# Attention and FP4 feed-forward on one core: output tiles in three PSUM banks, six residual buffers, and other places and lengths for the last two pairs' key sums

## The chip, the cores and the metric

The kernel runs on one core of a Trainium2 chip. The metric is device time in microseconds (us). The kernel before has a median of 3647.8 us over three runs (3647.26 to 3649.82).

## The reference

x is (8, 1024, 512), eight batches. Everything is float32.

```python
xn = _layernorm(x, axis=-1)
x = x + _L0_attn_ref(xn, W_attn, b_attn, W_proj, b_proj) + _L0_ffn_ref(xn, w_gate, w_up, w_down)

# attention: 16 heads of 32, causal
qkv = x @ W_attn + b_attn
att = jnp.einsum('bhqd,bhkd->bhqk', q, k) * HD ** (-0.5)
att = jax.nn.softmax(jnp.where(causal, att, -jnp.inf), axis=-1)
y = jnp.einsum('bhqk,bhkd->bhqd', att, v)
return y @ W_proj + b_proj

# feed forward: every operand rounded to blocks of 16 FP4 values with a common scale
h = jax.nn.silu(fp4_linear(x, w_gate)) * fp4_linear(x, w_up)
return fp4_linear(h, w_down)
```

## The kernel before, in words

The attention of all eight batches comes first (to about 2077 us of the span), then the feed-forward over 64 tiles of 128 rows. The change is in the attention, and its effects reach the first steps of the feed-forward.

A batch has three stages. In the first TensorE makes Q, K and V (line 1056, three products of rounded halves each). In the second it goes through eight pairs of heads, numbered 0 to 7 in the code. In the third, the output projection, it makes eight output tiles of 128 rows, "P0" to "P7" (line 1227). Each output tile is the sum over four groups of heads; a group is one matmul of the program and two instructions in the trace. Groups 0 to 2 need pairs 0 to 5, group 3 needs pairs 6 and 7.

**A pair.** TensorE computes the transposed scores of one key tile after the other (kt = 0 to 7, L1113). ScalarE writes their exponentials (L967 and L970). TensorE multiplies them with V (`times_v`, L1139). GpSimd adds the exponentials of the key tiles up: L613 adds tiles 0 and 1, and L615 adds tiles 2, 3, ... one by one. ScalarE copies the first 128 columns (L962). `denominators(p)` then multiplies these sums with ones on TensorE (L1151), and where GpSimd added only `summed(p)` tiles, it adds the remaining tiles' exponentials with further matmuls (L1158). For pairs 0 to 5 GpSimd adds all eight tiles. For pair 6 it adds five (kt = 0 to 4), for pair 7 three. The sums of pairs 1 and 3 lie in `xs`, those of all others in `stage`. So pair 7's first sum waits until the denominators of pair 6 have read `stage`.

For pairs 0 to 6 the denominators are issued in the middle of the next pair's steps, and their inverse goes through DMAs. For pair 7 they come last: VectorE takes the reciprocal from PSUM directly (L709) and divides (L720).

**The order around the projection.** All engines but SP issue in an order written out in the code. On TensorE, after the denominators of pair 7: the transposes of three tiles of the next batch's x (L1014), groups 0 to 2 of P0 and P1, the transpose of the fourth x tile, group 3 of P0 and P1, then P2 and P3 whole, the transposes of a quantised weight unit (L1098, `transpose_unit`), P4 and P5, those of a second unit, P6 and P7, and then the next batch's Q and K. P_k lies in bank k mod 2 of `ps_dense`, so P2 waits until VectorE has added P0 (`o_sum`).

On VectorE: four normalisations of the next batch's x (L645) in the middle of pair 7, the divisions of pair 6, the reciprocal and divisions of pair 7, `low_of_x` of the four x tiles (L651), and then `add(k)` for k = 0 to 7 (L731), with the quantisation of two weight units in between: after `add(0)` the scales of the first unit (L760 to L764), after `add(1)` its rounding (L770 to L774), after `add(2)` and `add(3)` the same for the second, after `add(4)` and `add(6)` their low halves (L780). The fourth `low_of_x` needs the fourth transpose. `transpose_unit` needs the end of the rounding (L774) of its unit, and for the second also the low half of the first.

`add(k)` also needs x plus the bias: ScalarE's queue loads a tile of x into one of two buffers (L935), and GpSimd adds the bias (L603). The first two loads are issued once the denominators of pair 7 are done, each later one after `add(k)` has freed its buffer.

In the last batch there is no next x to normalise and transpose; a tile of the feed-forward's x is quantised instead (L1360, L1553), and SP loads 18 weight blocks after `add(1)`.

Of the kernel before, what the change touches and what calls it, by code (L numbers as in the profile page):

```python
# [44 lines left out]
def attention(nc, ctx, banks, memory, shared, x, w_attn, b_attn, w_proj, b_proj, w_gate, w_up, w_down, qk_scratch, ones_scratch,  # L45
# [27 lines left out]
    ST_RING, SLOTS, XR = 3, 4, 4  # L73
# [10 lines left out]
    def summed(p):  # L84

        return ST if p < PAIRS - 2 else RINGED if p < PAIRS - 1 else 3
# [5 lines left out]
    SUMS0 = [sum(summed(k) - 1 for k in range(p)) for p in range(PAIRS)]  # L92
    SUMS = SUMS0[-1] + summed(PAIRS - 1) - 1
# [72 lines left out]
    stack01 = sb("stack01", [P, 2, 4, S], F32R)  # L166
    arena = sb("arena", [P, 2, KC, S], F32R)
# [73 lines left out]
    res_in = [sem(f"a_res_in{i}") for i in range(2)]  # L241
# [11 lines left out]
    ONE = 1  # L253
    LOOPED = [*x_in, bn_part, bn_tile, var_eps, rstd, normed, kept, d_full, t_full, t_hi, t_lo, qk_hi, qk_lo, *qk_out,
# [4 lines left out]
    LOADS = 7  # L259

# [9 lines left out]

    def bank(kind, i):
        return ps_dense[:, DN[kind, i] % 2]
# [9 lines left out]

    X_SUMS = (1, 3)
    SUMMED_IN = {p: max((k for k in range(p) if (k in X_SUMS) == (p in X_SUMS)), default=None) for p in range(PAIRS)}

    def sums(p, h):
        return both_sums(p)[:, h]

    def both_sums(p):
        if p in X_SUMS:  # L290
            return xs[:, :, :].rearrange("p (h a) n -> p h (a n)", h=2)
        return stage[:, :, :, :].rearrange("p h a n -> p h (a n)")
# [95 lines left out]

    def batches(eng, body):

        with eng.Fori(0, B - 1) as b:
            body(b, False)
        body(B - 1, True)
# [177 lines left out]
    def gpsimd(pool):  # L571
# [25 lines left out]
        def body(b, final):  # L597
            for t in range(XR, ST):
                inv_std(b, t)

            def x_and_bias(t):
                pool.wait_ge(res_in[t % 2], ONE + b * (ST // 2) * DMA + (t // 2 + 1) * DMA)
                nc.gpsimd.tensor_tensor(res[:, t % 2], res[:, t % 2], bp[:, :], ALU.add).then_inc(o_res, 1)  # L603

            def sum_up(p, kt):

                pool.wait_ge(st_exp, ONE + b * PAIRS * NPARTS + p * NPARTS + PART0[kt + 1])
                if kt > 1:
                    pool.wait_ge(summed_up, ONE + b * SUMS + SUMS0[p] + kt - 1)
                both = both_sums(p)  # L610
# [19 lines left out]
        batches(pool, body)  # L630

    def vector(dve):
# [45 lines left out]
        def body(b, final):  # L678
# [44 lines left out]
            def add(k):  # L723
# [7 lines left out]
                nc.vector.tensor_tensor(ob[:, k % 2], bank("P", k), res[:, k % 2], ALU.add).then_inc(o_sum, 1)  # L731
# [146 lines left out]
    def scalar(act):  # L878
# [14 lines left out]
        def body(b, final, rest):  # L893
# [37 lines left out]
            def load(k):  # L931

                t = OUT[k]
                act.wait_ge(o_sum, ONE + b * ST + max(k - 1, 0))
                act.dma_start(res[:, k % 2], x[b, t * P:(t + 1) * P, :]).then_inc(res_in[k % 2], DMA)  # L935
# [8 lines left out]
            for p in range(PAIRS):  # L944
                for kt in range(ST):
# [7 lines left out]
                    if kt == RINGED:  # L953
# [8 lines left out]
                        nc.scalar.activation(both_sums(p)[:, :, 0:P], exps(0)[:, :, 0:P], ACT.Copy).then_inc(first_sums, 1)  # L962
# [16 lines left out]
            for k in range(2):  # L979
                load(k)  # L980
# [6 lines left out]
            for k, t in enumerate(OUT):  # L987
                act.wait_ge(o_sum, ONE + b * ST + k + 1)
                act.dma_start(acc[b, t * P:(t + 1) * P, :], ob[:, k % 2]).then_inc(o_out[k % 2], DMA)
                if k + 2 < ST:  # L990
                    load(k + 2)
# [14 lines left out]
    def tensor(pe):  # L1006
# [20 lines left out]
        def body(b, final):  # L1027
            def emptied(kind, i):

                n = DN[kind, i] - 2  # L1030
# [6 lines left out]
                s, per = {"QK": (qk_lo, NQK), "V": (v_done, ST), "P": (o_sum, ST)}[k]  # L1037
# [105 lines left out]
            def denominators(p):  # L1143
                pe.wait_ge(summed_up, ONE + b * SUMS + SUMS0[p] + summed(p) - 1)
# [4 lines left out]
                for s in range(2):  # L1149
                    for h in range(2):  # L1150
                        last = nc.tensor.matmul(by_tile(den_bank(p)[y_rows(h, s)]), ones[:, :], by_tile(sums(p, h))[:, s::2],  # L1151
                                                start=True, stop=summed(p) == ST)
                for kt in range(summed(p), ST):
# [80 lines left out]
            for k in range(2):  # L1234
                pe.wait_ge(y_div, ONE + b * PAIRS * 2 + (PAIRS - 2 + k) * 2)
# [6 lines left out]
            for k in range(ST):  # L1242
                if k < 2:
# [23 lines left out]

    def x_read(eng):
# [3 lines left out]
    shared.wgu_in, shared.wd_in = wgu_in, wd_in  # L1272
    shared.all_quantised, shared.all_added, shared.projected, shared.x_read = all_quantised, all_added, projected, x_read
# [3 lines left out]
def feed_forward(nc, ctx, memory, shared, x, F, acc, wq, out):  # L1277
# [280 lines left out]
    def tensor(pe):  # L1558
# [26 lines left out]
        def step(t, first=False, second=False, last=False):  # L1585
            pe.wait_ge(xt_lo, t + 1)
            if first:
                pe.wait_ge(shared.wgu_in, len(PIECES) * DMA)
            else:
# [103 lines left out]
```

## Time and profile before

| | us |
|---|---|
| median of the runs | 3647.8 |
| the profiled execution, its own time | 3647.5 |
| its span, from the first to the last instruction | 3645.7 |
| mean granted TensorE clock | 0.997 of full speed |
| TensorE busy | 3597.6 (99%) |
| VectorE busy | 2610.7 (72%) |
| GpSimd busy | 1078.4 (30%) |

A busy share says little here, since matmuls overlap in the records. What counts is the stretch between the last pair of one batch and the first Q of the next, which comes once in each of the eight batches. The rows below show it in the second batch, where it runs from about 488 to 536 us. The same steps in the first batch stand between 234 and 282 us, in the eighth between 2024 and 2077 us.

### The profile page before, as it was taken

The page shows a single profiled execution, that of the slowest core. Times are in us where ns is not written, and L with a number is a line of the kernel's source. Part 1 is how long each engine was busy: PE and PEld are TensorE (multiplying, and loading weights), DVE is VectorE, ACT ScalarE, POOL GpSimd, SP SyncE. Part 2 cuts the span into 40 slices and gives each one's busy share as a digit, 9 for nine tenths or more (in the row PEclk, how much of TensorE's full clock was granted, in tenths as well). Part 3 has the DMA queues.
Part 4 walks back from the last instruction along what each step waited for, and adds up shares of the span by engine and source line. Part 5 has one row for each costly group of instructions (what it writes and reads, how often), then busy time and mean ns, then how long its engine had stood idle before and what let it go on. Part 6 is the DMA issues. An engine that isn't in the chain of part 4 may idle for free.

```text
span 3645.7 us, 55788 instructions
## 1 busy us (share of the span) xinstructions
PE 3597.6 (99%) x20748; PEld 2604.6 (71%) x20748; DVE 2610.7 (72%) x3834; ACT 1193.0 (33%) x2249; POOL 1078.4 (30%) x542
## 2 busy tenths in 40 slices
PE   8999999999999999999999999999999999999999
PEld 6557557566566575575565588888888888888887
DVE  6776766766767767767667577777777777777776
ACT  2542533533524515425325322222222222222222
POOL 0760952833825717608518300000000000000000
PEclk9999999999999999999999999999999999999999
DMA  6525436336255255254355500111011101110110
GB/s 195 133 77 183 110 115 177 83 119 181 64 168 150 66 186 129 80 183 101 120 167 156 202 26 29 35 35 32 29 35 35 32 29 35 35 32 29 35 35 29
DMA packets 180445, 336.13 MB, mean 92 GB/s; under 512 B 42688, under 2 KB 50368, under 8 KB 179392
## 3 DMA queue, kind: packets, MB, share of 16 engines
q1 hardware_dynamic: 156096, 280.47, 27.1%
q10 hardware_dynamic: 24192, 53.49, 4.3%
q8 instruction: 108, 1.77, 0.2%
q14 instruction: 49, 0.40, 0.0%
HBM read 213.92 MB, written 118.43 MB: 91 GB/s over the span
## 4 chain that ended last, share of the span: by engine, by line
PE 90%; issue 3%; POOL 2%; DVE 2%; DMA 1%; ACT 1%; SPq 0%; POOLq 0%; ACTq 0%; DVEq 0%
PE f_ps L1570 26%; PE ps_dense L1056 13%; PE f_ps_o L1582 13%; PE ps_st L1113 8%; PE ps_s L1081 5%; PE ps_dense L1227 5%; PE ps_y L1139 4%; PE ps_dense L1139 3%; PE ps_dense L1081 2%; PE ps_dense L1151 2%; PE f_ps L1562 1%; POOL stage L615 1%; PE ps_st L1122 1%; PE ps_s L1086 1%; POOL stage L613 1%
## 5 line engine op out<-in xcount | busy, mean ns | idle before, releaser
L1570 PE MATMUL f_ps<-wgu,xqt 128*128 128x512 f32 (+1 forms) x4608 | 992.7, 373 | 1.4 <-DVE xqt L1430 1.4
L1570 PEld LDWEIGHTS f_ps<-wgu,xqt 128*128 128x128 f32 x4608 | 842.5, 188 | 122.7 <-DVE xqt L1430 1.7
L967 ACT ACTIVATE pt<-ps_st 128x512 f32<-128x512 f32 (+3 forms) x1152 | 540.8, 525 | 489.9 <-PE ps_st L1113 335.3
L683 DVE TENSOR_REDUCE mx<-ps_s 128x1 f32<-128x640 f32 (+3 forms) x512 | 524.1, 1024 | 164.2 <-PE ps_s L1086 163.6
L1582 PE MATMUL f_ps_o<-wd,hqt 128*128 128x512 f32 x2112 | 513.4, 396 | 0.2 <-DVE hqt L1456 0.2
L1582 PEld LDWEIGHTS f_ps_o<-wd,hqt 128*128 128x128 f32 x2112 | 392.6, 189 | 79.5 <-DVE hqt L1456 0.6
L1056 PE MATMUL ps_dense<-arena,wa 128*128 128x512 f32 x1536 | 384.3, 400 | 0.0
L615 POOL TENSOR_TENSOR stage<-stage,pt 128x1536 f32<-128x1536 f32 (+2 forms) x128 | 378.9, 2960 | 16.6 <-ACT pt L967 6.3
L613 POOL TENSOR_TENSOR stage<-pt 128x1792 f32<-128x1792 f32 x48 | 192.7, 4014 | 615.9 <-ACT pt L967 563.9
L1056 PEld LDWEIGHTS ps_dense<-arena,wa 128*128 128x128 f32 x1536 | 281.9, 189 | 58.0 <-issue 3.8
L683 DVE TENSOR_REDUCE mx<-ps_dense 128x1 f32<-128x128 f32 (+3 forms) x424 | 204.4, 482 | 90.5 <-PE ps_dense L1086 90.5
L1113 PE MATMUL ps_st<-arena 98*128 98x512 f32 (+3 forms) x768 | 254.8, 401 | 4.0 <-DMA arena<-mr 2.1
L1113 PE MATMUL ps_st<-stack 98*128 98x512 f32 (+3 forms) x768 | 254.6, 397 | 0.4 <-ACT pt L967 0.2
L1227 PE MATMUL ps_dense<-wp,yt 128*128 128x512 f32 x512 | 227.5, 594 | 2.7 <-DVE rob L731 2.3
L1517 ACT ACTIVATE silu<-f_ps 128x512 f32<-128x512 f32 (+1 forms) x192 | 106.9, 557 | 369.1 <-PE f_ps L1570 369.1
L929 ACT ACTIVATE stage<-ps_dense,bqk 128x512 fp32r<-128x512 f32 x128 | 87.9, 687 | 351.6 <-PE ps_dense L1056 343.0
L1512 ACT ACTIVATE ha<-ht 128x1408 f32<-128x1408 f32 x63 | 87.1, 1383 | 325.3 <-DVE ht L1353 325.3
L1449 DVE TENSOR_TENSOR h<-silu,f_ps 128x512 f32<-128x512 f32 (+1 forms) x192 | 122.7, 639 | 95.6 <-ACT silu L1517 91.8
L1056 PE MATMUL ps_dense<-wa,arena 128*128 128x512 f32 x768 | 188.2, 395 | 0.0
L1113 PEld LDWEIGHTS ps_st<-arena 98*128 98x128 f32 x768 | 130.9, 193 | 77.3 <-ACT pt L967 41.3
L1227 PEld LDWEIGHTS ps_dense<-wp,yt 128*128 128x128 f32 x512 | 94.0, 190 | 113.8 <-issue 102.8
L736 DVE SCALAR_TENSOR_TENSOR stage<-ps_dense,bqk,stage 128x512 fp32r<-128x512 f32 x128 | 95.9, 749 | 105.7 <-ACT stage L929 105.7
(145 smaller groups left out, 5295.1 us busy)
## 6 DMA issues: line engine op xcount, KB each, us to landing
qk_scratch<-stage SPq DMA_DIRECT2D x128, 512.0 KB, 2.8
stack<-qk_scratch SPq DMA_DIRECT2D x192, 256.0 KB
arena<-qk_scratch SPq DMA_DIRECT2D x192, 256.0 KB
xs<-in_L_attn_x SPq DMA_DIRECT2D x64, 256.0 KB, 3.9
rob<-in_L_attn_x ACTq DMA_DIRECT2D x64, 256.0 KB, 2.9
acc_scratch<-rob ACTq DMA_DIRECT2D x64, 256.0 KB, 2.1
xt<-in_L_attn_x SPq DMA_DIRECT2D x64, 256.0 KB, 2.6
at<-acc_scratch SPq DMA_DIRECT2D x64, 256.0 KB, 2.7
```

Of the source, the lines that this page charges most:

```text
L613: nc.gpsimd.tensor_tensor(both[:, :, cols], exps(0)[:, :, cols], exps(1), ALU.add).then_inc(summed_up, 1)
L615: nc.gpsimd.tensor_tensor(both[:, :, cols], both[:, :, cols], exps(kt), ALU.add).then_inc(summed_up, 1)
L683: nc.vector.tensor_reduce(mx[:, h * ST + q:h * ST + q + 1], scores_bank(p, n)[:, 0:(q + 1) * P], axis=AX.X, op=ALU.max, negate=True).then_ ...
L967: nc.scalar.activation(exps(kt)[:, heads[0], q - kt * P:q - kt * P + n], ps_st[:, w % ST_RING, 0:n], ACT.Exp, scale=SCALE).then_inc(st_exp, 1)
L1056: last = nc.tensor.matmul(bank(*use), left(lh, k), right(rh, k), start=n == 0, stop=n == len(terms) - 1)
L1081: nc.tensor.matmul(out[:, k0:k1], qs, stack(p)[0:KS, 2 + h, k0:k1], start=True, stop=k1 < keys)
L1113: last = nc.tensor.matmul(ps_st[:, w % ST_RING, j * n:(j + 1) * n], stack(p)[0:KM, 2 + h, kt * P:(kt + 1) * P], stack(p)[0:KM, h, q:q + n] ...
L1139: last = nc.tensor.matmul(by_tile(y_bank(p)[y_rows(h, s), y_cols(kt, s)]), v_head(kt, p, h), exps_of_parity(kt, h, s), start=kt == 0, stop ...
L1227: last = nc.tensor.matmul(bank("P", k), yt[:, g, t * P:(t + 1) * P], wp[:, g, :], start=g == 0, stop=g == G - 1)
L1449: nc.vector.tensor_tensor(h[:, f:f + n], silu[:, c, 0:n], ps[:, SLOT[c], 1, 0:n], ALU.mult).then_inc(h_mul, 1)
L1570: last = nc.tensor.matmul(ps[:, SLOT[c], gu, 0:n].rearrange("p (j n) -> p j n", n=P), xqt[:, a, k], wgu[:, b, gu * FC + f // P:gu * FC + ( ...
L1582: last = nc.tensor.matmul(ps_o[:, :], hqt[:, a, k], wd[:, b, k], start=i == 0, stop=i == len(terms) - 1)
```

## The change

Four things change.

- **Three banks.** P_k goes to bank k mod 3 of `ps_dense[0]`, `ps_dense[1]` and the second half of `ps_s`. TensorE issues groups 0 to 2 of P0, P1 and P2 ahead of the fourth x transpose. P3 is the first that waits for `add(0)`. This holds in all eight batches.
- **Six residual buffers.** In all but the last batch, x tiles are loaded into six buffers, the two of `rob` and four in `stage`. Six loads are issued at once after the denominators of pair 7, and the last two after `add(0)` and `add(1)`.
- **Sums.** In all but the last batch, pair 6's sums lie in `left01`, which is what pairs 4 and 5 have left in `stack01`. So pair 7's first sum no longer waits for the denominators of pair 6. Pair 7 has five tiles summed in place of three.
- GpSimd's batches are written out in line and no longer in a loop, and the feed-forward's first matmuls wait also for `add(5)` of the last batch, since they use the third bank.

```diff
+    ST_RING, SLOTS, XR, RES = 3, 4, 4, 6
-    def summed(p):
-        return ST if p < PAIRS - 2 else RINGED if p < PAIRS - 1 else 3
+    def summed(p, final):
+        return ST if p < PAIRS - 2 else 3 if p == PAIRS - 1 and final else RINGED
...
+    left01 = memory.over("left01", [P, 2, 4, S], F32, "stack01")
...
+    def res_tile(k, final):
+        i = res_place(k, final)
+        return res[:, i] if i < 2 else stage[:, :, :, :].rearrange("p a c n -> p (a c) n")[:, i - 2]
+    def res_place(k, final):
+        return k % 2 if final else k % RES
...
+    OUT_BANKS = 3
     def bank(kind, i):
+        if kind == "P":
+            return [ps_dense[:, 0], ps_dense[:, 1], ps_s[:, QC:S]][i % OUT_BANKS]
...
+    def sums_place(p, final):
+        return 1 if p in X_SUMS else 2 if p == PAIRS - 2 and not final else 0
+    def summed_in(p, final):
+        return max((k for k in range(p) if sums_place(k, final) == sums_place(p, final)), default=None)
...
-                if SUMMED_IN[p] is not None:
-                    pool.wait_ge(den_full, ONE + b * PAIRS + SUMMED_IN[p] + 1)
-                for kt in SUM_ORDER[:summed(p) - 1]:
+                if summed_in(p, final) is not None:
+                    pool.wait_ge(den_full, ONE + b * PAIRS + summed_in(p, final) + 1)
+                for kt in SUM_ORDER[:summed(p, final) - 1]:
                     sum_up(p, kt)
...
-            for k in range(2):
+            for k in range(2 if final else RES):
                 load(k)
...
+                if kind == "P" and i >= OUT_BANKS:
+                    pe.wait_ge(o_sum, ONE + b * ST + i - OUT_BANKS + 1)
+                    return
...
-            for k in range(2):
-                pe.wait_ge(y_div, ONE + b * PAIRS * 2 + (PAIRS - 2 + k) * 2)
+            for k in range(OUT_BANKS):
+                pe.wait_ge(y_div, ONE + b * PAIRS * 2 + (PAIRS - 2 + min(k, 1)) * 2)
                 emptied("P", k)
                 output(k, range(G - 1))
             if not final:
                 transpose_x(b + 1, XR - 1)
...
-                if k < 2:
+                if k < OUT_BANKS:
                     output(k, [G - 1])
```

TensorE's queue in the first batch, from the denominators of pair 7 to the first `transpose_unit`. Before (`ps_st<-ident,xs` are the x transposes, `ps_dense<-wp,yt` the output tiles, `ps_y<-ident,pt` the weight unit; a matmul here is two instructions of the trace):

```order
L1151 MATMUL ps_s<-stage,ones 32x512 [waits a_first_sums,a_summed_up]
L1151 MATMUL ps_s<-stage,ones 32x512 x3
L1158 MATMUL ps_s<-pt,ones 32x256 x2
L1158 MATMUL ps_s<-pt,ones 32x384 x2
L1158 MATMUL ps_s<-pt,ones 32x256 x4
L1158 MATMUL ps_s<-rob,ones 32x128 x2
L1158 MATMUL ps_s<-rob,ones 32x256 x2
L1158 MATMUL ps_s<-rob,ones 32x128 x6
```

After, the same place:

```order
L1180 MATMUL ps_s<-stage,ones 32x512 [waits a_first_sums,a_summed_up]
L1180 MATMUL ps_s<-stage,ones 32x512 x3
L1187 MATMUL ps_s<-rob,ones 32x128 x2
L1187 MATMUL ps_s<-rob,ones 32x256 x2
L1187 MATMUL ps_s<-rob,ones 32x128 x6
```

The eight matmuls on the exponentials of tiles 3 and 4 are gone, and the wait on `a_summed_up` is now for four sums and not for two. Further down on TensorE, before:

```order
L1227 MATMUL ps_dense<-wp,yt 128x512 [waits a_v_done,a_y_div,a_den_copy]
L1227 MATMUL ps_dense<-wp,yt 128x512 x2
L1227 MATMUL ps_dense<-wp,yt 128x512 [waits a_v_done,a_y_div]
L1227 MATMUL ps_dense<-wp,yt 128x512 x2
L1014 MATMUL ps_st<-ident,xs 128x128 [waits a_normed,a_t_lo]
L1014 MATMUL ps_st<-ident,xs 128x128 x3
L1227 MATMUL ps_dense<-wp,yt 128x512 [waits a_y_div]
L1227 MATMUL ps_dense<-wp,yt 128x512
L1227 MATMUL ps_dense<-wp,yt 128x512 [waits a_o_sum]
L1227 MATMUL ps_dense<-wp,yt 128x512 x3
L1227 MATMUL ps_dense<-wp,yt 128x512 [waits a_o_sum]
L1227 MATMUL ps_dense<-wp,yt 128x512 x3
L1098 MATMUL ps_y<-ident,pt 128x128 [waits a_q_q,a_q_lo]
```

After:

```order
L1256 MATMUL ps_dense<-wp,yt 128x512 [waits a_v_done,a_y_div]
L1256 MATMUL ps_dense<-wp,yt 128x512 x2
L1256 MATMUL ps_s<-wp,yt 128x512 [waits a_s_max,a_y_div]
L1256 MATMUL ps_s<-wp,yt 128x512 x2
L1036 MATMUL ps_st<-ident,xs 128x128 [waits a_normed,a_t_lo]
L1036 MATMUL ps_st<-ident,xs 128x128 x3
L1256 MATMUL ps_dense<-wp,yt 128x512 [waits a_y_div]
L1256 MATMUL ps_dense<-wp,yt 128x512
L1256 MATMUL ps_s<-wp,yt 128x512
L1256 MATMUL ps_dense<-wp,yt 128x512 [waits a_o_sum]
L1256 MATMUL ps_dense<-wp,yt 128x512 x3
L1127 MATMUL ps_y<-ident,pt 128x128 [waits a_q_q,a_q_lo]
```

Three matmuls of P2 now stand ahead of the fourth x transpose, where before there were none of them; `transpose_unit` still comes after P3. VectorE's queue has the same instructions in the same order in both.

## Rows read from the trace of the kernel before

**Rows 1.** The page: the chain of work that ended last, by engine.

```profile
PE 90%; issue 3%; POOL 2%; DVE 2%; DMA 1%; ACT 1%; SPq 0%; POOLq 0%; ACTq 0%; DVEq 0%
```

**Rows 2.** Who TensorE waited for, whole span (total us, times, longest us).

```profile
PE ps_dense L1227 <- DVE rob L731: 2.3, 8, 0.3
```

**Rows 3.** Timeline of TensorE, pair 7 (start us, duration us, what).

```profile
501.69 0.62 PE L1151 MATMUL ps_s<-stage,ones 128*32 128x512 f32 x2
505.02 1.53 PE L1014 MATMUL ps_st<-ident,xs 128*128 128x128 f32 x12
506.38 5.32 PE L1227 MATMUL ps_dense<-wp,yt 128*128 128x512 f32 x12
511.54 0.60 PE L1014 MATMUL ps_st<-ident,xs 128*128 128x128 f32 x4
511.97 1.88 PE L1227 MATMUL ps_dense<-wp,yt 128*128 128x512 f32 x4
514.15 7.13 PE L1227 MATMUL ps_dense<-wp,yt 128*128 128x512 f32 x16 [0.29 <-DVE rob L731]
521.12 0.60 PE L1098 MATMUL ps_y<-ident,pt 128*128 128x128 f32 x4
```

**Rows 4.** Timeline of GpSimd: sums of pair 7, a bias addition.

```profile
488.90 1.02 POOL L593 TENSOR_TENSOR mv<-mv,small 128x4 f32<-128x4 f32 x1
492.56 4.02 POOL L613 TENSOR_TENSOR stage<-pt 128x1792 f32<-128x1792 f32 x1 [2.63 <-PE ps_dense L1158]
496.65 3.46 POOL L615 TENSOR_TENSOR stage<-stage,pt 128x1536 f32<-128x1536 f32 x1
...
523.94 1.42 POOL L603 TENSOR_TENSOR rob<-rob,bp 128x512 f32<-128x512 f32 x1 [2.46 <-DMA rob<-in_L_attn_x]
```

**Rows 5.** Groups of GpSimd's instructions by shape (total us, mean ns | idle before).

```profile
L615 POOL TENSOR_TENSOR stage<-stage,pt 128x1280 f32<-128x1280 f32 x40 | 117.0, 2925 | 4.1
L615 POOL TENSOR_TENSOR stage<-stage,pt 128x1024 f32<-128x1024 f32 x40 | 95.3, 2382 | 3.5
```

**Rows 6.** Timeline of ScalarE: last exponentials of tile 1, and of tile 2, pair 7.

```profile
490.46 0.49 ACT L967 ACTIVATE pt<-ps_st 128x384 f32<-128x384 f32 x1
...
494.14 1.15 ACT L967 ACTIVATE pt<-ps_st 128x512 f32<-128x512 f32 x3 [2.70 <-PE ps_st L1113]
```

**Rows 7.** Timeline of TensorE and VectorE: denominators of pair 6, begin and end.

```profile
490.45 1.06 PE L1151 MATMUL ps_dense<-stage,ones 128*32 128x512 f32 x8
...
492.50 0.69 DVE L700 COPY rob<-ps_dense 128x512 f32<-128x512 f32 x1 [3.14 <-PE ps_dense L1158]
```

**Rows 8.** Timeline of VectorE, from the end of pair 7.

```profile
498.64 1.76 DVE L645 TENSOR_SCALAR xs<-xs,mv 128x512 f32<-128x512 f32 x1
505.20 3.36 DVE L709 RECIPROCAL rob<-ps_s 128x512 f32<-128x512 f32 x1 [0.21 <-PE ps_s L1158]
510.11 1.89 DVE L651 TENSOR_TENSOR arena<-ps_st,arena 128x512 fp32r<-128x512 f32 x3
513.41 0.68 DVE L731 TENSOR_TENSOR rob<-ps_dense,rob 128x512 f32<-128x512 f32 x1
519.32 0.69 DVE L774 TENSOR_TENSOR pt<-pt 128x512 f32<-128x512 f32 x1
524.27 1.65 DVE L771 SCALAR_TENSOR_TENSOR pt<-pt 128x512 f32<-128x512 f32 x1
527.16 0.68 DVE L780 TENSOR_TENSOR pt<-ps_y,pt 128x512 fp32r<-128x512 f32 x1
```

**Rows 9.** All normalisations (duration ns min/median/max, first and last start).

```profile
L645 DVE TENSOR_SCALAR xs<-xs,mv x64: 533/538/3444, 14.2 to 1824.4; 128x512 f32<-128x512 f32 x64
```

**Rows 10.** Timeline of TensorE, the last batch's projection.

```profile
2042.64 5.32 PE L1227 MATMUL ps_dense<-wp,yt 128*128 128x512 f32 x12
2048.37 9.14 PE L1227 MATMUL ps_dense<-wp,yt 128*128 128x512 f32 x20 [0.41 <-DVE yt L720]
...
2068.07 0.66 PE L1098 MATMUL ps_y<-ident,pt 128*128 128x128 f32 x4 [2.73 <-DVE pt L780]
```

More of the change, by code:

```diff
@@ L82, in attention @@
     TAIL = 2 * P * sum(ST - k for k in range(RINGED, ST))
-    def summed(p):
-        return ST if p < PAIRS - 2 else RINGED if p < PAIRS - 1 else 3
+    def summed(p, final):
+        return ST if p < PAIRS - 2 else 3 if p == PAIRS - 1 and final else RINGED
     SUM_ORDER = [*range(1, ST)]
     FREED = {0: 1, 1: 1, 2: 2, 3: 3, 4: 4}
-    SUMS0 = [sum(summed(k) - 1 for k in range(p)) for p in range(PAIRS)]
-    SUMS = SUMS0[-1] + summed(PAIRS - 1) - 1
+    SUMS0 = [sum(summed(k, False) - 1 for k in range(p)) for p in range(PAIRS)]
+    SUMS = SUMS0[-1] + summed(PAIRS - 1, False) - 1
     TILES = 2 * ST
@@ L240, in attention @@
     y_div = sem("a_y_div")
-    res_in = [sem(f"a_res_in{i}") for i in range(2)]
+    res_in = [sem(f"a_res_in{i}") for i in range(RES)]
     o_res = sem("a_o_res")
@@ L259, in attention, with res_turn @@
     LOADS = 7
+    def res_tile(k, final):
[3 more added lines that the diff above has]
+        return k % 2 if final else k % RES
+    def res_turn(b, k, final):
+        if final:
+            return b * 2 + k // 2 + 1
+        return b * 2 + k // RES + 1 if k % RES < 2 else b + 1
     LOADS_AFTER = {GROUP0 - 1: LOADS, 6: 1, 7: 1, 8: 1, 9: 1, 10: 2, 11: 1}
@@ L283, in attention, with sums, both_sums @@
     X_SUMS = (1, 3)
[L284 to L292, printed above, removed]
+    def sums_place(p, final):
+        return 1 if p in X_SUMS else 2 if p == PAIRS - 2 and not final else 0
+    def summed_in(p, final):
+        return max((k for k in range(p) if sums_place(k, final) == sums_place(p, final)), default=None)
+    def sums(p, h, final):
+        return both_sums(p, final)[:, h]
+    def both_sums(p, final):
+        return [stage[:, :, :, :].rearrange("p h a n -> p h (a n)"),
+                xs[:, :, :].rearrange("p (h a) n -> p h (a n)", h=2),
+                left01[:, :, 3]][sums_place(p, final)]
     def by_tile(a):
@@ L387, in attention @@
     NEEDS.update({("V", t): t + 1 for t in range(ST)})
[L389 to L393, printed above, removed]
     def batches_in_line(body):
@@ L609, in sum_up @@
                     pool.wait_ge(summed_up, ONE + b * SUMS + SUMS0[p] + kt - 1)
-                both = both_sums(p)
+                both = both_sums(p, final)
                 cols = slice(kt * P, S)
@@ L628, in body @@
                 x_and_bias(t)
-        batches(pool, body)
+        batches_in_line(body)
     def vector(dve):
@@ L730, in add @@
                 filled(dve, b, "P", k)
-                nc.vector.tensor_tensor(ob[:, k % 2], bank("P", k), res[:, k % 2], ALU.add).then_inc(o_sum, 1)
+                nc.vector.tensor_tensor(ob[:, k % 2], bank("P", k), res_tile(k, final), ALU.add).then_inc(o_sum, 1)
             def low_of_qk(i):
@@ L933, in load @@
                 t = OUT[k]
-                act.wait_ge(o_sum, ONE + b * ST + max(k - 1, 0))
-                act.dma_start(res[:, k % 2], x[b, t * P:(t + 1) * P, :]).then_inc(res_in[k % 2], DMA)
+                act.wait_ge(o_sum, ONE + b * ST + max(k + 1 - (2 if final else RES), 0))
+                act.dma_start(res_tile(k, final), x[b, t * P:(t + 1) * P, :]).then_inc(res_in[res_place(k, final)], DMA)
             for i in range(2):
@@ L989, in body @@
                 act.dma_start(acc[b, t * P:(t + 1) * P, :], ob[:, k % 2]).then_inc(o_out[k % 2], DMA)
-                if k + 2 < ST:
-                    load(k + 2)
+                if k + (2 if final else RES) < ST:
+                    load(k + (2 if final else RES))
                 if k == 0:
@@ L1150, in denominators @@
                     for h in range(2):
-                        last = nc.tensor.matmul(by_tile(den_bank(p)[y_rows(h, s)]), ones[:, :], by_tile(sums(p, h))[:, s::2],
-                                                start=True, stop=summed(p) == ST)
-                for kt in range(summed(p), ST):
+                        last = nc.tensor.matmul(by_tile(den_bank(p)[y_rows(h, s)]), ones[:, :], by_tile(sums(p, h, final))[:, s::2],
+                                                start=True, stop=summed(p, final) == ST)
+                for kt in range(summed(p, final), ST):
                     for s in range(2):
```

19 lines of the change are left out of this document (13 added, 6 removed).

## The prediction, made before the changed kernel ran

> **What bounds the kernel now.** I read the chain of work that ended last, then TensorE's waits, then the engines' timelines around the end of a batch. The chain is 90% TensorE [rows 1], so an edit pays only if it shortens what TensorE does or waits for. The only wait that the third bank can remove is TensorE's on `add(0)`, and it is booked with 2.3 us over eight batches [rows 2]. In the timeline it is a little more: the four instructions from 511.97 at 0.43 us each would end at 513.69, and the next start at 514.15 [rows 3]. That is 0.46 us a batch. The reader is to see how tight the neighbours are. The denominators of pair 7 start at 501.69, and GpSimd's last sum had ended at 496.65 + 3.46 = 500.11 [rows 3, 4]: 1.6 us of slack. The first `transpose_unit` starts at 521.12, and the rounding that it needs ended at 519.32 + 0.69 = 520.01 [rows 3, 8]: 1.1 us of slack. The change uses up both.
>
> **Step A, the denominators of pair 7 (seven batches).** Gain: eight matmuls less. Pair 6's denominators have exactly the list that pair 7's will have. They ran from 490.45 to VectorE's start at 492.50, 2.05 us [rows 7]; pair 7's ran from 501.69 to 505.20, 3.51 us [rows 3, 8]. So 1.46 us is saved.
>
> Cost: two more sums stand ahead. The exponentials of tile 1 are ready at 490.46 + 0.49 = 490.95, and GpSimd is free at 488.90 + 1.02 = 489.92 [rows 4, 6], so the first sum can start at 491.0 instead of 492.56, the part that waited for pair 6's denominators. It ends at 495.0. Tile 2's exponentials come at 494.14 + 1.15 = 495.29 [rows 6]; its sum runs from 495.35 to 498.82. The sums of tiles 3 and 4 take 2.92 and 2.38 us [rows 5] with 0.08 us between, so the last ends at about 504.3. TensorE had nothing else left at 501.69 and issues in order: it waits 2.65 us. Behind it stand the transposes of x and the whole projection. Net A = 2.65 - 1.46 = +1.2 us.
>
> **Step B, the first weight unit (seven batches).** The third bank puts six instructions (2.6 us) ahead of the fourth x transpose. VectorE's `low_of_x` of that tile comes ahead of `add(0)`, and everything of VectorE behind `add(0)` moves with it. From the first x transpose at 505.02, TensorE before: first `transpose_unit` at 521.12, 16.1 us later [rows 3]. After: 1.36 us of transposes (506.38 - 505.02), 18 instructions at 5.16/12 = 0.43 us, 7.74 us, to the fourth transpose; 1.87 us from there to `add(0)` (513.41 - 511.54); 6.60 us from `add(0)` to the end of the rounding (520.01 - 513.41) [rows 3, 8]. Together 17.57. Is VectorE itself free by then? It starts the reciprocal when the denominators end (505.20) and had done three `low_of_x` at 512.00, 6.8 us later [rows 8]; the fourth transpose comes after 9 us. So `transpose_unit`, which stays behind P3, has to wait for the rounding, and B = +1.5 us; the 0.46 us gap is already inside these figures. P3 itself doesn't wait: `add(0)` ends at 11.65, and P3 starts at 12.1.
>
> The second `transpose_unit` follows 17 instructions of 0.43 us (four transposes count as one) after the first, 7.3 us, at 24.9 on this scale. It needs the first unit's low half, which ended 14.43 us after `add(0)` (527.84 - 513.41), at 25.4. But in this stretch an L771 took 1.65 us beside a bias addition of GpSimd at 523.94 [rows 4, 8]. That addition followed a load that `add(2)` freed, and with six buffers it is gone by then. So 0 to 0.5 us, and I take 0. After it TensorE runs P6 and P7 as before, and the delay reaches Q and K of the next batch in full.
>
> **Step C, VectorE and GpSimd beside each other.** A normalisation takes 0.54 us alone, and up to 3.44 [rows 9]. In the second batch the first one is issued at 498.64, under the sum that ends at 500.11, and ends at 500.40 [rows 4, 8]: it waits for the end of GpSimd's instruction. Before, nothing of GpSimd stood behind this sum. Now two sums do. If a normalisation gets in between two sums, it delays the second by 0.54 us. Bounds from these rows: nothing (GpSimd is never held up) to 1.9 us (all four go ahead, the later ones 0.45 us apart). I take one in each of the two gaps, +1.1 us. The Trainium skill, SBUF — State Buffer, in the section on the two separate sides, says that the two engines share one pair of ports as an exclusive lock which is held for a whole instruction, by whichever starts first. By that rule, the row on the normalisation agrees, and the delay goes in both directions, so C would not be zero; it doesn't say who is next in a queue.
>
> **Other edits, at nothing.** Six loads in ScalarE's queue take some 2.6 us ahead of its x copies; those are wanted only by `low_of_x` after the reciprocal and the divisions, 5 us later. They also don't shorten a wait of TensorE, since only 2.3 us in all hung on `add` [rows 2]. Pair 6's sums start up to 1 us earlier, and its denominators did not wait for them. GpSimd's batches in line: it sits idle at each batch's start. The feed-forward's wait for `add(5)`: that is two tiles before TensorE gets there.
>
> **The last batch.** Its sums and buffers are as before; only the bank changes. P2's first groups run from about 2047.8 to 2050.4 instead of the wait until 2048.37, so group 3 of P0 starts 2.0 us later than at 2048.37 [rows 10]. `add(0)`, its loads and the roundings all move by 2.0. TensorE reaches the first `transpose_unit` at 2056.4 and waits for its rounding. The second was bound by VectorE already, 2.73 us of waiting for the low half at 2068.07 [rows 10], and that chain, from `add(2)` over a load, starts 2.0 later. So +2.0 us; bounds 1 (loads slow for reasons of their own) to 3.
>
> **Sum.** 7 x (1.2 + 1.5 + 1.1) + 2.0 = 28.6 us. The span of the profiled execution is 3645.7, and its own time 3647.5, 0.3 under the median. 3647.5 + 28.6 = 3676.1; by the median 3676.4. I forecast 3676 us, slower by 0.8%.
>
> **Rivals.** Each by the same sum, from the median.
> - No port effect: C = 0. For it: no row shows GpSimd held up for long. 7 x 2.7 + 2 = 21, 3669 us.
> - All four normalisations go ahead of the sums: C = 1.9. For it: back to back they start before their predecessor has ended. 7 x 4.6 + 2 = 34, 3682 us.
> - Only the wait at the denominators: B is zero because VectorE gains its time back, for instance with fewer collisions in the first rounding too. Against it: the load that `add(0)` triggers, and its bias addition, come at the same distance as before. 7 x 2.3 + 1 = 17, 3665 us; with C = 0, 3657.
> - Faster: TensorE finds the sums ready, so that the 1.46 us saved counts, and VectorE's later rounding stays hidden. It decides by the time at which GpSimd's fourth sum ends: from 501.7 on it costs. 7 x (-1.46 - 0.46) - 1 = -14, 3633 us. Against it: 4.0 + 3.5 + 2.9 + 2.4 us of sums don't fit between 491.0 and 501.7, in any batch.
> - The change doesn't act as it says, because some other wait hides it: no change, 3648.
>
> **How the numbers follow.** Forecast 0.38, no port effect 0.25, all four ahead 0.16, denominators alone 0.14, no change 0.04, faster 0.03. About 0.2% (7 us) is what a measurement of this kernel can tell from none. The first four are all slower by more than that: 0.93. Range: the lower end 3660 takes in the case without port effect with a batch term of 1.6 in place of 2.7; the upper end 3686 has all four normalisations and 0.5 us at the second `transpose_unit`. The range leaves out the last two cases and part of the fourth.
>
> **What would show it.** On TensorE, in seven batches, a wait for GpSimd's L637 sum at the denominators of 2.6 us or more (right: A and C; its size above 2.65 is C), and a wait for VectorE's rounding ahead of `transpose_unit` of 1.8 to 2.0 us (right: B). The sum of tile 1 of pair 7 starts 1.5 us earlier. The wait of P3 for `add(0)` is gone. The time from one batch to the next grows by 3.8 us. Wrong would be: denominators that start as early as before, or a `transpose_unit` without a wait.

## The result, and the profile after

The changed kernel takes 3682.8 us (median of four runs, 3679.1 to 3691.3), the kernel before 3648.8 beside it. The ratio is 1.0097, with a 95% interval of 1.0081 to 1.0113: slower by 1%. The forecast was 3676 us, with a range of 3660 to 3686. The profiled execution has a span of 3678.9 us, 33.2 more than before.

TensorE's waits in the changed kernel. The columns are those of [rows 2]; L637 is GpSimd's sum, L796 the end of a unit's rounding (L774 before), L802 its low half (L780 before).

```profile
PE ps_y L1127 <- DVE pt L796: 15.9, 8, 2.0
PE ps_s L1180 <- POOL stage L637: 15.1, 7, 2.2
...
PE ps_dense L1180 <- POOL stage L637: 3.6, 8, 0.5
PE ps_y L1127 <- DVE pt L802: 3.3, 1, 3.3
```

The reader is to see that the wait for `add(0)` of [rows 2] is gone and that two larger ones have come: eight ahead of the first `transpose_unit`, and seven at pair 7's denominators. In the chain of work that ended last GpSimd and VectorE have 3% each now, from 2% [rows 1]:

```profile
PE 90%; POOL 3%; DVE 3%; ACT 1%; DMA 1%; issue 1%; SPq 0%; ACTq 0%; POOLq 0%; DVEq 0%
```

TensorE in the timeline of the second batch; it answers to [rows 3].

```profile
506.01 1.26 PE L1168 MATMUL ps_y<-rob,v 128*32 128x128 f32 x20
509.45 1.07 PE L1180 MATMUL ps_s<-stage,ones 128*32 128x512 f32 x8 [2.18 <-POOL stage L637]
510.34 1.05 PE L1187 MATMUL ps_s<-rob,ones 128*32 128x128 f32 x20
511.32 1.53 PE L1036 MATMUL ps_st<-ident,xs 128*128 128x128 f32 x12
512.69 5.32 PE L1256 MATMUL ps_dense<-wp,yt 128*128 128x512 f32 x12
517.84 2.74 PE L1256 MATMUL ps_s<-wp,yt 128*128 128x512 f32 x6
520.41 0.60 PE L1036 MATMUL ps_st<-ident,xs 128*128 128x128 f32 x4
520.85 1.88 PE L1256 MATMUL ps_dense<-wp,yt 128*128 128x512 f32 x4
522.57 1.02 PE L1256 MATMUL ps_s<-wp,yt 128*128 128x512 f32 x2
523.43 3.60 PE L1256 MATMUL ps_dense<-wp,yt 128*128 128x512 f32 x8
529.04 0.95 PE L1127 MATMUL ps_y<-ident,pt 128*128 128x128 f32 x4 [2.01 <-DVE pt L796]
529.78 5.01 PE L1256 MATMUL ps_dense<-wp,yt 128*128 128x512 f32 x8
534.62 3.60 PE L1256 MATMUL ps_s<-wp,yt 128*128 128x512 f32 x8
```

Both waits stand where the prediction put them. The last two rows show something that it didn't have: eight instructions of P4 take 5.01 us, the same eight of P5 3.60. The busy times by window say why (window, length, then busy time and count of TensorE, its weight loads, VectorE, ScalarE and GpSimd, the granted clock, DMA share, GB/s):

```profile
520.00:529.00 9.00, 7.02 (x20) 3.04 (x18) 7.02 (x12) 1.23 (x2) 4.10 (x5) 1.00 0.54 165
529.20:532.60 3.40, 3.40 (x8) 1.85 (x8) 3.16 (x8) 0.63 (x1) 1.06 (x1) 0.50 0.21 77
533.00:537.00 4.00, 4.00 (x11) 1.81 (x10) 2.68 (x5) 0.31 (x1) 0.00 (x0) 1.00 0.32 117
```

The granted clock was 0.50 (1.2 GHz) from 529.2 to 532.6, right behind the wait of 2.01 us, and 1.00 (2.4 GHz) around it. I call this a clock fall below.

GpSimd's sums for pair 7, one row each, and VectorE's four normalisations in the same stretch; they answer to [rows 4, 8].

```profile
496.09 4.01 POOL L635 TENSOR_TENSOR stage<-pt 128x1792 f32<-128x1792 f32 x1 [1.73 <-ACT pt L989]
500.36 3.48 POOL L637 TENSOR_TENSOR stage<-stage,pt 128x1536 f32<-128x1536 f32 x1 [0.26 <-ACT pt L989]
503.98 2.93 POOL L637 TENSOR_TENSOR stage<-stage,pt 128x1280 f32<-128x1280 f32 x1
507.06 2.34 POOL L637 TENSOR_TENSOR stage<-stage,pt 128x1024 f32<-128x1024 f32 x1
...
501.94 2.19 DVE L667 TENSOR_SCALAR xs<-xs,mv 128x512 f32<-128x512 f32 x1
504.04 3.15 DVE L667 TENSOR_SCALAR xs<-xs,mv 128x512 f32<-128x512 f32 x1
507.12 2.56 DVE L667 TENSOR_SCALAR xs<-xs,mv 128x512 f32<-128x512 f32 x1
509.60 0.53 DVE L667 TENSOR_SCALAR xs<-xs,mv 128x512 f32<-128x512 f32 x1
```

### Where the 33.2 us are

A batch splits at two starts on TensorE: **T**, the first x transpose behind pair 7's denominators, and **Q**, the first matmul of the next batch. In [rows 3] T is at 505.02, above at 511.32. Means in us, worked out from the start times in each timeline, T to Q over the first seven batches and Q to T over the six stretches between them (the kernels with labels are those of the next section):

| | Q to T | T to Q |
|---|---|---|
| before | 224.24 | 30.33 |
| changed | 226.31 | 33.17 |
| e3, before with GpSimd in line | 224.94 | 30.31 |
| e1, changed with three tiles summed | 224.97 | 32.72 |
| e9, changed, P2 not ahead | 226.95 | 30.44 |
| e7, before with the bank alone | 224.24 | 29.79 |
| e10, four tiles summed, two buffers | 223.74 | 29.77 |

In the changed kernel T to Q is 31.96 or 31.99 in the two batches without a clock fall, and 33.64 to 33.66 in the five with one. So a fall costs 1.7 us and the rest is +1.6. Over the span: six stretches from Q to T at +2.07 (12.4), 1.0 from the span's start to the first T, seven from T to Q at +2.84 (19.9), and 3.2 in the last batch (0.6 before T, 2.6 after). The feed-forward was 3.2 us shorter, because the profile of the kernel before had one clock fall more in it. The sum is 33.3.

### The profile page after: what moved, and what is told of

Its sections match the earlier page's. It is cut to its first block, busy times and chain, and to the rows that moved or that the text cites. A ratio compares the mean times of both kernels' runs of the same rounds, so it can differ in the third digit from the quotient of the medians.

```text
span 3678.9 us, 55204 instructions
## 1 busy us (share of the span) xinstructions
PE 3599.6 (98%) x20636; PEld 2603.0 (71%) x20636; DVE 2632.2 (72%) x3834; ACT 1194.1 (32%) x2249; POOL 1113.9 (30%) x556
## 4 chain that ended last, share of the span: by engine, by line
PE 90%; POOL 3%; DVE 3%; ACT 1%; DMA 1%; issue 1%; SPq 0%; ACTq 0%; POOLq 0%; DVEq 0%
PE f_ps L1604 26%; PE ps_dense L1085 13%; PE f_ps_o L1616 13%; PE ps_st L1142 8%; PE ps_s L1110 6%; PE ps_dense L1168 4%; PE ps_dense L1256 4%; PE ps_y L1168 3%; POOL stage L637 3%; PE ps_dense L1110 2%; PE ps_dense L1180 2%; PE f_ps L1596 1%; PE ps_s L1256 1%; PE ps_st L1151 1%; ACT pt L989 1%; PE ps_s L1115 1%
## 5 line engine op out<-in xcount | busy, mean ns | idle before, releaser
L637 POOL TENSOR_TENSOR stage<-stage,pt 128x1536 f32<-128x1536 f32 (+2 forms) x121 | 354.6, 2931 | 20.5 <-ACT pt L989 6.6
L635 POOL TENSOR_TENSOR stage<-pt 128x1792 f32<-128x1792 f32 x41 | 164.8, 4020 | 596.4 <-ACT pt L989 576.8
L1256 PE MATMUL ps_dense<-wp,yt 128*128 128x512 f32 x384 | 180.3, 618 | 0.0
L1390 DVE SCALAR_TENSOR_TENSOR hd<-ha,ht 128x1408 f32<-128x1408 f32 (+1 forms) x65 | 104.2, 1603 | 91.9 <-ACT ha L1546 91.2
```

The lines of the kernel that those rows point to most:

```text
L1256: last = nc.tensor.matmul(bank("P", k), yt[:, g, t * P:(t + 1) * P], wp[:, g, :], start=g == 0, stop=g == G - 1)
```

## The experiments

The letters: A is the wait at pair 7's denominators, B the wait at the first `transpose_unit`, K the clock falls, L what GpSimd's code in line costs. Each time stands beside runs of the kernel before on the same chip; their median was 3647.2 us for e1 to e8, 3647.0 for e9 and 3647.6 for e10.

### e1: three tiles summed for pair 7

```diff
-        return ST if p < PAIRS - 2 else 3 if p == PAIRS - 1 and final else RINGED
+        return ST if p < PAIRS - 2 else 3 if p == PAIRS - 1 else RINGED
```

> The changed kernel with three key tiles summed for pair 7 in every batch, in place of five; banks, buffers, places and in-line GpSimd stay. My theory has four parts in the changed kernel: A, TensorE waits 2.2 us at pair 7's denominators in seven batches, net +1.2 us each; B, 2.0 us ahead of the first transpose_unit, net +1.6 each; K, TensorE's granted clock falls to half for 3.4 us after that second wait in most batches, 1.7 us each; L, in line each GpSimd sum starts 0.07 us later, about 0.7 us a batch. Here A goes and B stays: no wait of TensorE for L637 at ps_s L1180, the wait for L796 stays at 2.0 us, and the time is 3682.8 - 7 x 1.2 = 3674. If the clock falls because of the wait at transpose_unit alone, it still falls at it in most batches; rival: it takes both waits within 20 us, then it falls in none and the time is 3664. Rival to A: the longer denominators cost more than the wait saves, 3683.

3672.0 us (3670.6 to 3674.1), ratio 1.0067 (1.0053 to 1.0081). Its waits:

```profile
PE ps_y L1127 <- DVE pt L796: 16.1, 8, 2.2
...
PE ps_dense L1180 <- POOL stage L637: 4.2, 9, 0.5
```

The 15.1 us at `ps_s L1180` are gone and the wait at `transpose_unit` stays. Q to T falls from 226.31 to 224.97, so A is 1.34 us a batch. A clock fall follows the wait at `transpose_unit` in three of seven batches, so it doesn't take two waits. A is shown, and its rival falls.

### e2: two output banks

```diff
-    OUT_BANKS = 3
+    OUT_BANKS = 2
...
-                shared.last_bank_read(pe)
```

> The changed kernel with two output banks instead of three (and no wait of the feed-forward for add(5)); five tiles summed, six buffers, in-line GpSimd stay. B goes and A stays: the wait ahead of transpose_unit is 0, the wait of 2.2 us at pair 7's denominators stays, P2 again waits about 0.5 us for add(0). 3682.8 - 7 x 1.6 - 1.0 for the last batch = 3671 if the clock falls stay (they would then follow the wait at the denominators), and about 3661 if they were due to the wait at transpose_unit. Rival: B isn't the bank's doing but comes from the six loads in ScalarE's queue; then the wait of 2.0 us stays and the time is 3682.

3667.6 us (3665.4 to 3671.2), ratio 1.0057 (1.0044 to 1.0071).

```profile
PE ps_s L1180 <- POOL stage L637: 15.3, 7, 2.2
...
PE ps_dense L1256 <- DVE rob L753: 4.2, 9, 1.5
```

The wait at `transpose_unit` is gone, so B belongs to the bank edit and not to the six loads. The wait at the denominators is still there, now with a clock fall behind it in three of seven batches; in the changed kernel it had none. And a wait for VectorE's additions reached 1.5 us: VectorE comes late here, which e10 explains.

### e3 and e4: GpSimd in line, and in a loop

e3 is the kernel before with `batches_in_line(body)` for GpSimd. e4 is the changed kernel with the loop:

```diff
-        batches_in_line(body)
+        with pool.Fori(0, B - 1) as b:
+            body(b, False)
+        body(B - 1, True)
```

> The kernel before with GpSimd's batches written out in line, nothing else. By L: the idle time between two sums of a pair is 0.14 us instead of 0.07, TensorE waits up to 0.5 us at denominators of some pairs, and the time is 0.7 us a batch longer, 3648.8 + 5 = 3654. Rival: in line is free (it sits idle at each batch's start), 3649, and the 0.7 us a batch come from left01 or the loads.

> The changed kernel with GpSimd's first seven batches in a loop again. By L: 3682.8 - 7 x 0.7 - 7 x 0.2 (three gaps less ahead of pair 7's denominators) = 3676; waits at ps_dense L1180 for L637 of 3.6 us in total go to below 1. Rival: no change, 3683.

e3: 3652.1 us (3648.7 to 3653.9, 11 runs), ratio 1.0011 (1.0002 to 1.0020). Three sums of a pair in its timeline:

```profile
441.69 9.06 POOL L615 TENSOR_TENSOR stage<-stage,pt 128x1536 f32<-128x1536 f32 x3 [0.26 <-ACT pt L967]
```

These are 0.14 us apart. In the kernel before the same three are 0.08 us apart:

```profile
461.01 8.94 POOL L615 TENSOR_TENSOR stage<-stage,pt 128x1536 f32<-128x1536 f32 x3
```

What in the in-line code costs the 0.06 us was not taken apart. The delays add up over a pair's seven sums, and TensorE waits at denominators, 4.1 us in the span:

```profile
PE ps_dense L1151 <- POOL stage L615: 4.1, 8, 0.5
```

Q to T grows by 0.70 us in e3. So L is shown, 0.7 us a batch, and in-line code that I had booked at nothing costs about 5 us.

e4: 3682.9 us (3676.1 to 3689.7), ratio 1.0099 (1.0084 to 1.0114), no faster than the changed kernel. Its trace has L's part back: the small waits at `ps_dense` are gone from its waits, and in the second and third batch, without a clock fall between Q and T, Q to T was 225.6 and 225.4, against 226.0 and 225.9. In the fifth, without one either, it was 226.8 against 226.7. The smaller gaps between pair 7's sums gave nothing: from the last score matmul to T it took 6.15 us, and 6.08 in the changed kernel. The second sum waits for exponentials in both, and the part on C below says what holds the other two. And it had seven clock falls in the first seven batches where the changed kernel's profile had five. In time e4 says nothing of L.

### e5: a version to beat both

```diff
-        return ST if p < PAIRS - 2 else 3 if p == PAIRS - 1 and final else RINGED
+        return ST if p < PAIRS - 2 else RINGED if p < PAIRS - 1 else 3 if final else 4
...
-            for k in range(OUT_BANKS):
+            for k in range(2):
...
-                if k < OUT_BANKS:
+                if k < 2:
                     output(k, [G - 1])
```

and GpSimd in the loop of e4.

> A version to beat both: the changed kernel with GpSimd in a loop, four key tiles summed for pair 7 (not five), and the third bank used by P2 without moving P2's groups ahead of the fourth x transpose. With the sum of tile 3 the last, GpSimd ends about 0.1 us after the point at which TensorE gets there, so a wait of 0.2 us, and four matmuls (eight instructions, about 0.7 us) are saved; P2 no longer waits (0.46 us). Seven times -1.0 us: 3647 - 7 = 3640. No wait at transpose_unit, and by K (the clock falls only behind a wait of TensorE of about 2 us) no clock fall at these places. Rival: the saved matmuls ran beside others and save nothing, and VectorE's normalisations, held up by the sum, delay add(0): 3647 to 3650.

3644.3 us (3641.2 to 3651.6, 11 runs), ratio 0.9994 (0.9985 to 1.0003): no change that could be told, between the expectation and its rival. Its waits:

```profile
PE ps_y L1129 <- DVE pt L798: 1.8, 6, 0.4
```

The saved matmuls do save: from the last score matmul to T it takes 4.14 us, and 4.79 in the kernel before. But VectorE comes late again, so `transpose_unit` waits up to 0.4 us, which gives back part of that. I put it down to the normalisations at first; e10 says otherwise. The profiled execution was the slowest of the eleven, with a clock fall that e8 comes back to.

### e6: the first transpose_unit after P4

```diff
-                if k == 3:
+                if k == 4:
                     transpose_unit(one)
```

> The changed kernel with the first transpose_unit issued after P4 in place of P3. By B the unit's rounding is ready by then (P4 takes 3.4 us, the wait was 2.0), so the wait goes, and the time falls by 7 x 1.6 + 1 = 12 us and by the clock falls behind that wait (5 to 7 of 1.7 us): 3660 to 3663. The wait at pair 7's denominators stays, with a clock fall behind it in some batches. Rival: the wait comes back at the second transpose_unit, which needs the first unit's low half; then 3675 or more.

3678.3 us (3675.8 to 3683.1), ratio 1.0085 (1.0072 to 1.0099). The rival held.

```profile
PE ps_s L1180 <- POOL stage L637: 15.4, 7, 2.4
PE ps_y L1127 <- DVE pt L802: 15.4, 8, 5.3
```

The wait for the rounding (L796) is gone and one of 1.4 us for the first unit's low half (L802) has come at the second `transpose_unit`. VectorE's row of work is the limit of this stretch; TensorE can mostly choose only where it waits. In the first batch, where the clock fall was over before T, T to Q took 31.41 us, 0.6 less than in the changed kernel without a fall. The wait at the denominators had a clock fall behind it in all seven batches.

### e7: the third bank alone

The kernel before, with P2 and P5 in the third bank and nothing moved ahead; as in the changed kernel, the feed-forward's first matmuls wait for `add(5)`:

```diff
     def bank(kind, i):
+        if kind == "P":
+            return [ps_dense[:, 0], ps_dense[:, 1], ps_s[:, QC:S]][i % 3]
         return ps_dense[:, DN[kind, i] % 2]
...
+                if kind == "P" and i > 2:
+                    pe.wait_ge(o_sum, ONE + b * ST + i - 2)
+                    return
+                if kind == "P" and i == 2:
+                    pe.wait_ge(s_max, ONE + (b + 1) * PAIRS * TILES)
+                    return
```

> The kernel before with the third bank alone, P2's groups not moved ahead. It removes the wait of P2 for add(0), 0.46 us a batch, and nothing else: 3647 - 3 = 3644 at best. Rival: no change at all, because TensorE then waits the same time at the first transpose_unit, whose rounding ended only 1.1 us before.

3641.2 us (3639.2 to 3645.2, 11 runs), ratio 0.9985 (0.9976 to 0.9994). This version beats both kernels. T to Q falls from 30.33 to 29.79:

```profile
511.29 1.88 PE L1235 MATMUL ps_dense<-wp,yt 128*128 128x512 f32 x4
513.01 3.60 PE L1235 MATMUL ps_s<-wp,yt 128*128 128x512 f32 x8
```

P2 follows P1 without the gap of [rows 3]. 7 x 0.54 is 3.8 us. The last batch gains 1.0 more (from P0's first to P7's last matmul 31.3 us, before 32.4). The last 1.2 us of the difference in medians stay open.

### e8: the first transpose_unit after P2

e6's edit with `k == 2`.

> A measurement of K. The changed kernel with the first transpose_unit issued after P2 in place of P3, so that TensorE waits there 2.0 + 3.4 = 5.4 us. The waiting itself adds 7 x 3.4 = 24 us (less what the second transpose_unit gives back: none). If clock falls follow from waiting, a longer wait brings one in nearly every batch (7 of 7, against 5 of 7 in the changed kernel's profile), or longer ones: 3682.8 + 24 + 3 to 12 = 3710 to 3719. If the falls are chance, they are as before, at places that have nothing to do with the wait: 3707.

3714.3 us (3709.8 to 3717.6), ratio 1.0182 (1.0166 to 1.0197). TensorE waits 5.4 us:

```profile
PE ps_y L1127 <- DVE pt L796: 43.3, 8, 5.4
```

and the windows of the second batch, around that wait, are

```profile
529.00:534.00 5.00, 0.00 (x0) 0.00 (x0) 4.73 (x8) 0.63 (x1) 1.34 (x1) 1.00 0.69 220
534.20:537.60 3.40, 3.24 (x7) 1.92 (x8) 2.61 (x7) 0.61 (x1) 1.27 (x1) 0.50 0.23 82
538.00:542.00 4.00, 4.00 (x11) 1.72 (x10) 1.82 (x3) 0.60 (x1) 0.00 (x0) 1.00 0.07 26
```

The clock fell to 0.50 at this wait in eight of eight batches. With waits of 2.0 to 2.4 us, in the first seven batches of the changed kernel, e1, e2, e4, e6, e8 and e9, a fall followed 31 of 63. The 11 waits of 1.4 to 1.8 us (the seven of e6 at the second `transpose_unit`, the first one of the last batch in the changed kernel, e1 and e4, and the one of 1.53 us in e2) had none, and the kernel before and e7, which do not wait in these stretches, had none there in their first seven batches. The kernel before shows the same where it does wait. TensorE stood idle for 5.59 us at 1859.13, and in the windows around that

```profile
1853.00:1855.50 2.50, 0.53 (x3) 0.10 (x1) 0.00 (x0) 0.00 (x0) 0.00 (x0) 1.00 0.98 336
1855.80:1862.50 6.70, 3.37 (x10) 2.69 (x11) 5.30 (x10) 1.21 (x2) 0.00 (x0) 0.50 0.40 142
```

the clock fell during the wait. The same wait, for VectorE at the first scores of the last batch, is in all twelve profiles, 4.5 to 6.1 us long, with a fall at each. At the second `transpose_unit` of the last batch, a wait of 5.3 us (e6) and six of 2.9 to 3.3 us had a fall, four of 2.0 to 2.7 us none. The kernel's start and the feed-forward are not in these counts. One fall stands against a simple rule. In e5's second batch the clock was down for 10.2 us behind a wait of only 1.05 us:

```profile
486.81 0.73 PE L1144 MATMUL ps_st<-arena 98*128 98x512 f32 x2 [1.05 <-DMA arena<-mr]
...
487.60:497.70 10.10, 10.10 (x64) 4.48 (x68) 1.38 (x2) 4.48 (x9) 5.21 (x4) 0.50 0.06 13
```

So waits of 2.9 us and more brought a fall every time, and waits of 2 us in half of the cases. Which of these do, and what brought the one in e5, was not settled.

### e9: P2 not ahead

The two edits of e5 to `range(2)` and `k < 2` alone, on the changed kernel.

> The changed kernel with one edit: P2's groups 0 to 2 are not issued ahead of the fourth x transpose, but behind group 3 of P1, still in the third bank. If B is the place of these six instructions and not the bank, the wait ahead of transpose_unit falls from 2.0 us to 0.4 or less, the time from the first x transpose to transpose_unit from 17.7 to 16.0 us (15.5 in the kernel with the bank alone, 0.4 more because VectorE is behind after the normalisations), and the last batch gains 1 us. The wait at pair 7's denominators stays, with a clock fall behind it in some batches. 3682.8 - 7 x 1.7 - 1 = 3670, and 5 us less if the falls behind transpose_unit aren't replaced by others: 3665 to 3670. Rival: B is the bank or the loads; then 3683.

3663.2 us (3661.8 to 3665.5), ratio 1.0044 (1.0030 to 1.0058), 20 us less than the changed kernel. The first of its waits is

```profile
PE ps_s L1180 <- POOL stage L637: 15.2, 7, 2.2
```

and that at `transpose_unit` is gone from the longest ones. T to Q falls from 33.17 to 30.44, while Q to T is 0.64 longer, mostly by the clock falls ahead of T. So B is the place of six instructions, with the bank left as it is. A fall followed the denominators' wait in three of seven batches. T to `transpose_unit` is 15.7 to 16.6 us, not 15.5 as with the bank alone. In the seventh batch VectorE's scale instructions show where that comes from; the second takes 1.25 us, and 0.18 in the kernel before:

```profile
1804.38 0.68 DVE L782 TENSOR_REDUCE pt<-pt 128x32 f32<-128x512 f32 x1
1805.09 1.25 DVE L783 TENSOR_SCALAR pt<-pt 128x32 f32<-128x32 f32 x1
...
1803.80 2.50 POOL L625 TENSOR_TENSOR stage<-stage,bp 128x512 f32<-128x512 f32 x2
```

GpSimd is adding the bias to two of the six prefetched tiles; they end at 1806.30, the scale instruction at 1806.34. So not the normalisations, as the expectation had it.

### e10: four tiles summed, two buffers

e5 with the residual tiles in two buffers again:

```diff
-    ST_RING, SLOTS, XR, RES = 3, 4, 4, 6
+    ST_RING, SLOTS, XR, RES = 3, 4, 4, 2
...
     def res_turn(b, k, final):
-        if final:
-            return b * 2 + k // 2 + 1
-        return b * 2 + k // RES + 1 if k % RES < 2 else b + 1
+        return b * (ST // 2) + k // 2 + 1
```

> e5 with two residual buffers in place of six, for the question why VectorE is late in e2, e5 and e9. Their traces show the small scale instructions of the first unit (0.18 us alone) taking up to 1.25 us while GpSimd adds the bias to six tiles in a row; not the normalisations, as I had written for e9. If it is the six buffers, the time from the first x transpose to transpose_unit goes from 16.0 us in e5 to 15.5, as with the bank alone, without a wait, and the time is 7 x 0.4 = 3 us under e5's 3644: 3641, level with the bank alone or a little better. Rival: it is the normalisations behind the sums; then the 0.3 us of waiting stay, and the time is 3644.

3639.8 us (3636.3 to 3648.4, 11 runs), ratio 0.9981 (0.9972 to 0.9990). T to `transpose_unit` is 15.54 us in all seven batches, no wait is left there, and the scale instruction takes 0.18 us. T to Q is 29.77 us, and 30.21 in e5, so the six buffers cost 7 x 0.44 = 3.1 us there, by GpSimd's additions falling beside VectorE's scales. The medians are 4.5 us apart, but stand on two chips and their intervals overlap. Against the kernel before, Q to T is 0.50 and T to Q 0.57 us shorter, 7.5 us over seven batches, and the medians are 7.7 apart. This is the fastest kernel of the study, 0.2% under the one before; against e7, 3641.2, the difference is within the noise.

## Why the prediction was right

The time fell into the range 7 us above the point, and slower was forecast with 0.93. By its steps:

- **What bounds the kernel.** Right. The slack of 1.6 and 1.1 us that it read from the rows is what the change used up; e1 and e9 each give it back.
- **A, +1.2 us.** Right in mechanism and nearly in size. It put 13.35 us between the start of pair 7's first sum and the denominators; they came 13.36 us after it (496.09 to 509.45). From the last score matmul of pair 7 to T it took 4.79 us before and 6.08 after, so A is 1.3 us a batch. The sign that was asked for, a wait of 2.6 us or more, did not come: the list has 2.2. The list counts from the recorded end of the last matmul, and before, the denominators had started 0.27 us ahead of that end. Counted from the last score matmul they start 2.77 us later than before (4.22 us behind it, before 1.45), against the 2.65 of the prediction.
- **B, +1.5 us.** Right. T to `transpose_unit` was put at 17.57 us and is 17.72 (511.32 to 529.04). Without a clock fall B is +1.6.
- **The second `transpose_unit`, 0.** Right. The second L793 took 0.69 us, without a bias addition beside it, and TensorE did not wait there.
- **C, +1.1 us.** This term failed, in its size. What it describes came: one normalisation got in between each two sums, and each later one waited out GpSimd's next sum, 3.15 and 2.56 us for 0.54. The prediction had 0.54 us as the price that GpSimd pays for one normalisation ahead of a sum. In the changed kernel it paid nothing: its sums stand 0.14 us apart, exactly as in e3, where nothing presses between them. A normalisation that has waited for a sum ends only 0.28 us behind it, and GpSimd's next sum need not wait for all of that. Yet it does wait for VectorE, as the sums of tile 3 in e4 show. There GpSimd runs in the loop and issues it 0.08 us after the sum before. First batch, its sum and the normalisation, and the same sum in the second batch:

```profile
244.53 3.15 POOL L637 TENSOR_TENSOR stage<-stage,pt 128x1280 f32<-128x1280 f32 x1
244.44 0.46 DVE L669 TENSOR_SCALAR xs<-xs,mv 128x512 f32<-128x512 f32 x1
...
505.68 2.98 POOL L637 TENSOR_TENSOR stage<-stage,pt 128x1280 f32<-128x1280 f32 x1
```

Alone this sum takes 2.93 us. Over all profiles there are 56 batches with a normalisation ahead of it, which ended 0.28 to 0.49 us behind the sum before, and the sum ended 2.77 to 2.79 us after the normalisation in every one. So GpSimd is held up, for up to 0.22 us in these rows; a normalisation that was queued costs it 0.06 us in the loop, and in line the wider gap covers that. By the rule of the Trainium skill that was cited (SBUF — State Buffer, the section on the two separate sides), the one that comes second waits for the whole instruction of the other. The trace agrees in both directions, but for some 0.15 us by which the sum is ahead of the normalisation's recorded end. The rival "no port effect" was right about the time and wrong about the reason. VectorE paid as well, but in time that it had: its divisions of pair 6 (from 510.06) were done at 511.46, when the denominators were (its reciprocal starts at 511.50).
- **Six buffers, 0.** Right for the changed kernel, since P2's matmuls put VectorE's scales (from 523.60) behind the last of the six additions (ended at 522.71), and wrong as a price: e10 against e5 shows 3.1 us where the scales come earlier. I had looked at what the loads queue ahead of and not at when GpSimd's additions would run.
- **GpSimd in line, 0.** Wrong. I argued from the start of the batch, where it sits idle, and did not ask what becomes of the waits between two sums in each pair. +0.7 us a batch, shown by e3.
- **The last batch, +2.0.** From P0's first matmul, the first rounding ends 1.9 us later and the first `transpose_unit` starts 0.9 later, as worked out. The other 1.0 that I expected from the load chain did not come (its wait grew only from 2.73 to 3.26 us); a clock fall behind that wait, 1.6 us, stood in its place.
- **K** is not in the prediction. Five falls of 1.7 us in the first seven batches, 8.5 us in the profile. The times of the changed kernel follow its mean granted clock: 3679.1 us at 0.996, 3680.7 (the profiled one) at 0.995, 3684.9 at 0.994, 3691.3 at 0.992.

So the sum was right with two terms wrong: 7.7 us for C that did not come, and some 5 us for L and 8.5 for K that were missing. "No port effect" without L and K would have said 3669; the measured time is above it by those two. The point's closeness is in part luck; what carried the forecast is that A and B, 7 x 2.9 us as they came, both come from differences of a few tenths read off the rows.

## What to carry to other kernels

Work that is put ahead "while waiting" delays what stands behind it: here six matmuls delayed one transpose, and through VectorE's queue a wait further down that was four times the gap they filled. Before an edit for a wait of half a microsecond, read the slack at the next two waits. Take the parts of a change one by one: here the third bank alone was faster by 0.15% and the whole slower by 1%.

## What the runs showed of the hardware

- TensorE's granted clock fell from 1.00 to 0.50 behind waits of TensorE of 2.0 to 2.4 us in half of the cases (31 of 63), at waits of 2.9 to 6.1 us always (27 of 27, eight of them in e8), and behind waits of 1.4 to 1.8 us never (0 of 11), all in the attention behind its start; but it fell once for 10.2 us behind a wait of 1.05 us (e5). Each of the 31 falls lasted 3.4 us, and those from T to Q in the changed kernel cost 1.7 us. By these, a wait of 2 us cost about 2.8 us (an estimate, 2.0 + 31/63 x 1.7).
- A normalisation on VectorE (fp32, SBUF to SBUF, 0.54 us alone) that meets GpSimd's tensor_tensor ends only after it, after up to 3.45 us (e3). Even a scale instruction of 32 columns takes 1.25 us for 0.18 (e9). The other way round GpSimd waits too, but one normalisation cost its next sum only 0 to 0.22 us.
- GpSimd's dependent sums stand 0.14 us apart in the in-line code and 0.08 us apart in the loop (e3 against the kernel before). Which part of the code makes the difference was not taken apart.
